# Attention with group norm: exponentials turned unnormalised, a sixth group turned by DMA, tile pairs parted into heads and tails

## What is computed

```python
y = group_norm(x, 4 groups) * gn_gamma + gn_beta
q, k, v = split(einsum('bchw,dc->bdhw', y, w_qkv) + b_qkv)
scores = einsum('bnc,bcm->bnm', q, k) * C ** (-0.5)
w = softmax(scores, axis=-1)
a = einsum('bnm,bmc->bnc', w, v)
return x + einsum('bchw,dc->bdhw', a, w_out) + b_out
```

## Time and profile before

| what | us |
|---|---|
| runs | 144.53, 144.81, 147.99 |
| median | 144.81 |
| span of the profiled execution | 143.7 |
| TensorE busy | 133.6 |
| VectorE busy | 103.9 |
| ScalarE busy | 67.7 |
| GpSimd busy | 57.1 |

### The profile page before, as it was taken

How to read it: one execution, slowest core, us unless ns; L and a number is a source line. 1 busy time by engine, 2 the same in 40 slices (tenths; PEclk the granted TensorE clock), 3 DMA queues, 4 the chain that set the end, 5 groups by cost and what they waited for, 6 DMA issues and landing times.

```text
span 143.7 us, 1862 instructions
## 1 busy us (share of the span) xinstructions
PE 133.6 (93%) x589; PEld 94.4 (66%) x589; DVE 103.9 (72%) x201; ACT 67.7 (47%) x122; POOL 57.1 (40%) x66
## 2 busy tenths in 40 slices
PE   7999999997499979997999999999999999999990
PEld 7978579873367635665655556766776666768770
DVE  0597587799978999899496987898763787463402
ACT  3164858763266526543361364455843666353000
POOL 6032347963334666633355556433543213330000
PEclk9999999999999999999999999999999999999998
DMA  4940000000045976983598539973996001000211
GB/s 159 310 188 0 0 5 0 0 2 0 0 101 117 206 165 141 206 200 109 109 203 197 152 66 206 206 182 81 212 203 168 0 0 73 0 0 0 80 70 73
DMA packets 6154, 15.07 MB, mean 105 GB/s; under 512 B 1664, under 2 KB 1664, under 8 KB 6144
## 3 DMA queue, kind: packets, MB, share of 16 engines
q1 hardware_dynamic: 5856, 14.69, 41.3%
q10 hardware_dynamic: 288, 0.27, 0.5%
HBM read 2.36 MB, written 2.10 MB: 31 GB/s over the span
## 4 chain that ended last, share of the span: by engine, by line
PE 66%; DVE 14%; SPq 7%; issue 5%; ACT 4%; DMA 2%; DVEq 0%
PE mixed L765 22%; SPq L235 7%; PE scores L715 5%; PE scores L714 5%; PE turned L731 5%; PE scores L717 5%; DVE scores L527 5%; PE scores L773 4%; DVE crossed L552 4%; ACT probs L366 3%; PE mixed L760 3%; PE mixed L762 3%; PE mixed L761 3%; PE turned L661 2%; PE mixed L661 2%
## 5 line engine op out<-in xcount | busy, mean ns | idle before, releaser
L295 POOL TENSOR_SCALAR probs<-probs,inv_sum 128x1024 f32<-128x1024 f32 x32 | 35.9, 1122 | 63.7 <-DVE inv_sum L532 63.7
L527 DVE TENSOR_SCALAR_CACHE_REDUCE scores<-scores,key_bias 128x1024 f32<-128x1024 f32 x31 | 40.0, 1289 | 13.9 <-PE scores L717 13.8
L366 ACT ACTIVATE probs<-scores,neg_max 128x1024 f32<-128x1024 f32 x32 | 35.7, 1115 | 18.7 <-DVE scores L527 17.7
L765 PE MATMUL mixed<-crossed,v 128*128 128x512 f32 x80 | 37.7, 593 | 1.0 <-DMA crossed<-crossed 1.0
L714 PE MATMUL scores<-y_hi,z_hi 128*128 128x512 f32 x62 | 34.6, 558 | 0.3 <-DVE z_lo L489 0.3
L552 DVE STREAM_TRANSPOSE crossed<-probs 128x1024 f32<-128x1024 f32 x20 | 24.8, 1241 | 0.0
L715 PE MATMUL scores<-y_lo,z_hi 128*128 128x512 f32 x62 | 24.4, 394 | 0.0
L765 PEld LDWEIGHTS mixed<-crossed,v 128*128 128x128 f32 x80 | 14.1, 190 | 11.6 <-issue 11.0
L717 PE MATMUL scores<-y_hi,z_lo 128*128 128x512 f32 x62 | 19.3, 392 | 0.0
L714 PEld LDWEIGHTS scores<-y_hi,z_hi 128*128 128x128 f32 x62 | 11.7, 189 | 8.8 <-issue 5.7
L715 PEld LDWEIGHTS scores<-y_lo,z_hi 128*128 128x128 f32 x62 | 11.7, 189 | 7.0 <-issue 5.5
(11 more groups left out here) (147 smaller groups left out, 168.9 us busy)
## 6 DMA issues: line engine op xcount, KB each, us to landing
crossed<-crossed SPq DMA_DIRECT2D x80, 128.0 KB, 2.3
out_dram<-result SPq DMA_DIRECT2D x8, 256.0 KB, 2.5
xs<-in_x_dram SPq DMA_DIRECT2D x2, 512.0 KB, 6.4
xs<-in_x_dram SPq DMA_DIRECT2D x3, 256.0 KB, 5.0
xs<-in_x_dram ACTq DMA_DIRECT2D x1, 256.0 KB, 3.5
ws<-in_weights_dram SPq DMA_DIRECT2D x1, 256.0 KB, 3.7
vecs<-in_vectors_dram ACTq DMA_DIRECT2D x1, 3.0 KB, 3.9
```

Source lines behind the costliest of these rows:

```text
L295: pool.tensor_scalar(probs[:, i % RING, :], probs[:, i % RING, :], inv_sum[:, i:i + 1], 1.0, ALU.mult, ALU.mult).then_inc(s_probs, 1)
L366: act.activation(probs[:, i % RING, :], scores[:, i % 2, :], ACT.Exp, bias=neg_max[:, i:i + 1], scale=-1.0, accum_out=row_sum[:, i:i + 1]) ...
L527: dve.tensor_scalar(scores[:, i % 2, :], scores[:, i % 2, :], key_bias[:, b % 2, i:i + 1], None, ALU.subtract, ALU.min, accum_out=neg_max[ ...
L765: mm = pe.matmul(bank, v[:, b % 2, k, :], at, start=first, stop=final)
```

## The change

The flips and the turning of group 0 wait for the exponentials alone. Groups 0 to 6 stay unnormalised until after the mix: one reciprocal for each group (`inverse_sums`), its 512 values are kept in DRAM (`keep_rows`) and read back on all partitions (`spread_rows`), `scale` multiplies the mixed tile by them, and GpSimd adds `x` with the output bias (`residual`, `add_residual`). Group 7 is normalised as before. Group 6 is swapped by DMA instead of turned by TensorE. In groups 1 to 6 the first pair of tiles is mixed in float32; each of the other three is parted: ScalarE makes the head (`pair_head`), GpSimd the tail in place (`pair_tail`), TensorE does three fp32r matmuls for a tile. All values get head and tail (`value_copy`, now two activations, and `value_tail`). The statistics of batches 2 and 3 are made together in blocks 0 to 3, their group means at block 6. y, z, and the big buffers become tensors of their own. The core of the diff:

```diff
-SWAPPED = range(1, 6)
-SPLIT_GROUPS = (6, 7)
-HOME = (0, 1, 0, 1, 0, 1)
+SWAPPED = range(1, 7)
+LAST = GROUPS_OF_FOUR - 1
+WHOLE_PAIR = 0
+PAIRS = KT // 2
+PARTED = PAIRS - 1
 SWAP = 16 * SQ * SQ
-MIX = {4: [(0, 1)], 5: [(0, 1)], 6: [(0, 1)], 7: [(0, 1)], 8: [(0, 1)], 9: [(0, 1)], 10: [(0, 2)],
-       27: [(5, 2)], 28: [(5, 3)], 29: [(5, 2)], 30: [(5, 1), (6, 3)], 31: [(6, 5)]}
-for group in range(1, 5):
-    for k, tiles in enumerate((3, 2, 1, 2) if group % 2 else (1, 2, 3, 2)):
-        MIX.setdefault(4 * group + 7 + k, []).append((group, tiles))
+MIX = {4: [(0, 1)], 5: [(0, 1)], 6: [(0, 1)], 7: [(0, 1)], 8: [(0, 1)], 9: [(0, 1)], 10: [(0, 2)]}
+for group in SWAPPED:
+    for k in range(PAIRS):
+        MIX.setdefault(4 * group + 7 + k, []).append((group, 2))
+
+inverse_rows = nc.dram_tensor("inverse_rows", (GROUPS_OF_FOUR - 1, HALF), fp32)
...
+def keep_rows(group):
+    sp.wait_ge(s_inv, group + 1)
+    sp.dma_start(inverse_rows[group].rearrange("(p u) -> p u", u=QB),
+                 inv_sum[:, group, :]).then_inc(s_rows[group % 2], 16)
+
+def spread_rows(group):
+    sp.wait_ge(s_rows[group % 2], 16 * (group // 2 + 1))
+    if group > 1:
+        sp.wait_ge(s_scaled, group - 1)
+    sp.dma_start(inv_wide[:, group % 2, :],
+                 inverse_rows[group].partition_broadcast(128)).then_inc(s_wide[group % 2], 16)
...
 sp.wait_ge(s_flipped, QB * group)
-if group > 1:
+if group > 2:
     sp.wait_ge(s_mixed, KT * (group - 1))
 for k in range(SQ):
     for g in (0, 2, 1, 3):
         t = g ^ k
-        sp.dma_start(crossed[32 * t:32 * t + 32, group % 2, g * N:(g + 1) * N],
-                     crossed[32 * g:32 * g + 32, 2 + group % 2, t * N:(t + 1) * N]
+        sp.dma_start(home[group % 2][32 * t:32 * t + 32, g * N:(g + 1) * N].bitcast(fp32),
+                     flipped[group % 2][32 * g:32 * g + 32, t * N:(t + 1) * N]
                      ).then_inc(s_swapped[group % 2], 16)
...
-swap(1)
-for group in range(2, 6):
+keep_rows(0)
+spread_rows(0)
+for group in SWAPPED:
+    keep_rows(group)
     swap(group)
-    store(group - 2)
-for group in range(4, GROUPS_OF_FOUR):
+    spread_rows(group)
+    if group >= 2:
+        store(group - 2)
+for group in range(5, GROUPS_OF_FOUR):
...
+def value_tail(b):
+    pool.wait_ge(s_v, 3 * (b + 1))
+    if b >= 2:
+        pool.wait_ge(s_mixed, KT * HALVES * (b - 1))
+    pool.tensor_tensor(v_lo[:, b % 2, :, :], v[:, b % 2, :, :], v_hi[:, b % 2, :, :].bitcast(fp32),
+                       ALU.subtract).then_inc(s_v_lo, 1)
+
+def pair_tail(group, pair):
+    pool.wait_ge(s_head, pair_number(group, pair))
+    there = pair_at_home(group, pair)
+    pool.tensor_tensor(there, there.bitcast(fp32), pair_of_heads(pair).bitcast(fp32),
+                       ALU.subtract).then_inc(s_parted, 1)
...
+def residual(b):
...
+pool.tensor_scalar(xs[:, b, :], xs[:, b, :], out_bias[:, :], 1.0,
+                   ALU.add, ALU.mult).then_inc(s_residual, 1)
...
+def add_residual(group):
+    b, g = group // HALVES, group % HALVES
+    pool.wait_ge(s_scaled, group + 1)
+    pool.wait_ge(s_residual, b + 1)
+    pool.tensor_tensor(result[:, g, :], result[:, g, :], xs[:, b, g * HALF:(g + 1) * HALF],
+                       ALU.add).then_inc(s_result, 1)
...
-normalise(0, 0)
 rstd_of(1, 2, 2)
-normalise(0, 1)
 for b in range(BATCHES):
     for i in range(BLOCKS):
-        behind = 0 < b < BATCHES - 1 and i == 3
-        if behind:
-            y_tail(b + 1, 0)
+        n = BLOCKS * b + i
+        group, pair = (n - 6) // QB, (n - 6) % QB
+        if group in SWAPPED and pair != WHOLE_PAIR:
+            pair_tail(group, pair)
+        if b == 0 and i == 0:
+            normalised_input(1)
         if b == 0 and i in (2, 3):
             y_tail(1, i - 2)
-        if after(b, i, 2)[0] < BATCHES:
-            normalise(*after(b, i, 2))
-        if behind:
+        if i == 2:
+            value_tail(b)
+        if i == 5:
+            residual(b)
+        if b == 1 and i == 0:
+            rstd_of(2, 4, 3)
+        if 0 < b < BATCHES - 1 and i == 1:
+            normalised_input(b + 1)
+        if 0 < b < BATCHES - 1 and i == 3:
+            y_tail(b + 1, 0)
+        if 0 < b < BATCHES - 1 and i == 4:
             y_tail(b + 1, 1)
-        if 0 < b < BATCHES - 1 and i == 0:
-            rstd_of(b + 1, b + 2, b + 2)
-        if i == (0 if b == 0 else 1) and b + 1 < BATCHES:
-            normalised_input(b + 1)
         if i == 7 and b + 1 < BATCHES:
             z_tail(b + 1)
+        if n >= 12 and n % QB == 0:
+            add_residual((n - 12) // QB)
+        if n + 2 >= QB * LAST and n + 2 < BATCHES * BLOCKS:
+            normalise(n + 2)
+for pair in range(2, PAIRS):
+    pair_tail(LAST - 1, pair)
+add_residual(LAST - 2)
+add_residual(LAST - 1)
...
+act.activation(v[:, b % 2, lo:hi, :], tiles, ACT.Copy)
+act.activation(v_hi[:, b % 2, lo:hi, :], tiles, ACT.Copy).then_inc(s_v, 1)
...
+def pair_head(group, pair):
+    act.wait_ge(s_swapped[group % 2], swaps(group))
+    act.wait_ge(s_mixed, KT * (group - 1) + 2 * (pair + 1) if group > 1 else KT)
+    act.activation(pair_of_heads(pair), pair_at_home(group, pair).bitcast(fp32), ACT.Copy).then_inc(s_head, 1)
...
+        group, pair = (BLOCKS * b + i - 6) // QB, (BLOCKS * b + i - 6) % QB
+        if group in SWAPPED and pair != WHOLE_PAIR:
+            pair_head(group, pair)
         if after(b, i, 2)[0] < BATCHES:
             exponentials(*after(b, i, 2))
         if i == (1 if b == 0 else 2) and not last:
             y_head(b + 1)
+for pair in range(2, PAIRS):
+    pair_head(LAST - 1, pair)
...
-def inverse_sum(b, i):
-    dve.wait_ge(s_exp, BLOCKS * b + i + 1)
-    dve.reciprocal(inv_sum[:, i:i + 1], row_sum[:, i:i + 1]).then_inc(s_inv, 1)
+def inverse_sums(group):
+    first = group % HALVES * QB
+    dve.wait_ge(s_exp, QB * (group + 1))
+    dve.reciprocal(inv_sum[:, group, :], row_sum[:, first:first + QB]).then_inc(s_inv, 1)
+
+def last_inverse_sum(n):
+    dve.wait_ge(s_exp, n + 1)
+    dve.reciprocal(inv_sum[:, LAST, n % QB:n % QB + 1],
+                   row_sum[:, n % BLOCKS:n % BLOCKS + 1]).then_inc(s_inv_last, 1)
...
-dve.wait_ge(s_probs, n + 1)
+dve.wait_ge(s_exp, n + 1)
...
-def results(group):
+def scale(group):
     b, g = group // HALVES, group % HALVES
     dve.wait_ge(s_mixed, KT * (group + 1))
     if b >= 1:
         dve.wait_ge(s_stored[g], 16 * b)
-    dve.scalar_tensor_tensor(out=result[:, g, :], in0=mixed[:, g, :], scalar=out_bias[:, :],
-                             in1=xs[:, b, g * HALF:(g + 1) * HALF], op0=ALU.add,
-                             op1=ALU.add).then_inc(s_result, 1)
+    dve.wait_ge(s_wide[g], 16 * (b + 1))
+    dve.tensor_tensor(result[:, g, :].rearrange("p (u q) -> p u q", u=QB),
+                      mixed[:, g, :].rearrange("p (u q) -> p u q", u=QB),
+                      inv_wide[:, g, :].rearrange("p (q u) -> p u q", u=QB), ALU.mult).then_inc(s_scaled, 1)
...
+if (BLOCKS * b + i) % QB == 2 and (BLOCKS * b + i) // QB < LAST:
+    inverse_sums((BLOCKS * b + i) // QB)
...
-            results((BLOCKS * b + i - 11) // QB)
-        if ahead[0] < BATCHES:
-            inverse_sum(*ahead)
-        if b + 2 < BATCHES and i in (4, 5):
-            half_stats(b + 2, i - 4)
-            if i == 5:
-                channel_stats(b + 2, b + 3)
-        if 0 < b < BATCHES - 1 and i == 1:
-            dve.wait_ge(s_negated, b)
-            coefficients(b + 1, b + 2, b + 2, negated_mean[:, b + 1:b + 2])
-results(GROUPS_OF_FOUR - 2)
-results(GROUPS_OF_FOUR - 1)
+            scale((BLOCKS * b + i - 11) // QB)
+        if ahead[0] < BATCHES and BLOCKS * b + i + 2 >= QB * LAST:
+            last_inverse_sum(BLOCKS * b + i + 2)
+        if b == 0 and i < 4:
+            half_stats(2 + i // 2, i % 2)
+            if i == 3:
+                channel_stats(2, 4)
+        if b == 1 and i == 1:
+            dve.wait_ge(s_negated, 1)
+            coefficients(2, 4, 3, negated_mean[:, 2:4])
+scale(LAST - 1)
+last_result()
...
-pe.wait_ge(s_probs, n + 1)
+if n < QB:
+    pe.wait_ge(s_exp, n + 1)
+else:
+    pe.wait_ge(s_probs, n - QB * LAST + 1)
...
+pair = k // 2
+if group in SWAPPED and pair != WHOLE_PAIR and k % 2 == 0:
+    pe.wait_ge(s_parted, pair_number(group, pair))
 first, final = k == 0, k == KT - 1
-if group in SPLIT_GROUPS:
-    head, tail = PT_HI[group][:, k, :], PT_LO[group][:, k, :]
-    pe.matmul(bank, v_hi[:, k, :], head, start=first, stop=False)
-    pe.matmul(bank, v_hi[:, k, :], tail, start=False, stop=False)
-    mm = pe.matmul(bank, v_lo[:, k, :], head, start=False, stop=final)
-elif group in SWAPPED:
-    at = crossed[:, HOME[group], :].rearrange("p (g v u c) -> p v u g c", g=SQ, v=KT, u=QB)[:, k, :, :, :]
-    mm = pe.matmul(bank, v[:, b % 2, k, :], at, start=first, stop=final)
+if group == 0:
+    mm = pe.matmul(bank, v[:, 0, k, :], first_turned[:, k, :], start=first, stop=final)
+elif group == LAST:
+    pe.matmul(bank, v_hi[:, b % 2, k, :], last_head[:, k, :], start=first, stop=False)
```

(34 more changed lines are left out.)

209 lines of the change are left out of this document (115 added, 94 removed).

## The result

| kernel | median us (runs) | ratio to before, 95% interval | span of the profile |
|---|---|---|---|
| before | 144.94 (144.53 to 147.99) | | 143.7 |
| changed | 155.71 (155.18 to 156.36) | 1.074 [1.068, 1.080] | 154.0 |

The change makes the kernel 7.4% slower. The forecast was 154.3 us with 146.5 to 160: right in sign, 1.4 us low.

What follows compares the result with a forecast made beforehand. It took TensorE to bound the kernel before and late GpSimd tails to delay it after. First mix at 52.65, plus 76.2 of TensorE work and 21.05 of waits, gives 149.9; with 3.3 and 1.1, 154.3 us, range 146.5 to 160.

Steps and rivals of the forecast that it cites:

- What bounds, and the change of the bound: TensorE bounds before, 85.24 busy of 86.65 us; after, it waits for GpSimd's pair tails and at Z0, about 20 us.
- The tail: GpSimd's pair tail, two inputs and 1024 columns: 2.33 us each, within bounds of 1.12 and 2.56.
- The walk through the queues: Block by block from 11 through ScalarE, GpSimd and TensorE queues: waits of 21.05 us; blocks 15 to 23 take 32.55.
- First mix to last matmul: TensorE from first transfer-fed mix at 52.65 to last matmul at 149.9: 76.2 us of work plus 21.05 of waits.
- The start: Stretch up to the first transfer-fed mix: flip(7) ends about 39.0 instead of 40.2, so that mix starts at 52.65.
- eight reciprocals leave: VectorE in blocks 4 and 5: eight reciprocals, and statistics of 0.68 us each, are no longer there.
- the first transfer-fed mix at 52 to 54: Sign of the forecast on TensorE: the first mix fed by transfers starts at 52 to 54 us.
- A: Rival: tails ready before their block, TensorE stays the bound; 135 to 138 us, needs tails well under 1.6; chance 0.09.
- B: Rival: half of the coupling, heads or tails shorter, tails 1.75 to 2.0 us; time 142 to 147.5; chance 0.12.
- C: Rival: GpSimd's tails collide with VectorE's two-input work on GpSimd's port; at 2.56 a tail, 159 us; chance 0.07.
- D: Rival: gaps of 2.6 us lower TensorE's clock to 1.2 GHz, up to 7 us more before the end; 161; chance 0.04.
- clock 1.00: Sign of the forecast: TensorE's granted clock stays at 1.00, that is 2.4 GHz.

Runs made afterwards that it cites:

- half tails: Changed kernel with each GpSimd pair tail cut from 1024 to 512 columns, order kept, output not the reference's; 139.45 us, ratio 0.962 to before.

## Why the prediction was right, point by point

- **What bounds, and the change of the bound**: right. TensorE's waits went to pair tails and to Z0, by name, and the last chain is GpSimd's (34%) as much as TensorE's (33%).
- **The tail, 2.33 us from two rows of the same operation**: measured 2.374 and 2.380. The bounds 1.12 and 2.56 were far apart, and the value taken was 2% off. The Trainium skill (GPSIMD Engine Reference, section 3.1) led to an estimate of 2.2; the row decides, and the rule is 7% low here.
- **The walk through the queues**: right in kind, and in size within 3%. Blocks 15 to 23: 32.55 predicted, 33.50 measured. Each of the places that it named is in the trace: Z0 behind the tail, pair 2 of an odd group behind Z0's copy, pair 1 of an even group behind two copies (1.14 idle at 74.03, 1.2 predicted), and three tails in a row before the last group with idle times of 2.48, 0.64 and 0.65 (2.55, 0.95 and 0.95 predicted from start to start).
- **First mix to last matmul**: 97.25 predicted, 99.94 measured (50.69 to 150.63). Of the 2.7, tails 0.045 longer along a path with some 20 of them are 0.9, an estimate; the lower clock about 131 is 0.7. In block 19 the tail of pair 1 of group 3 waited 0.67 for its head, which stood behind an exponential and y's head, and started 4.18 us behind the last mix of group 2 where the walk had 3.75: 0.4. The other 0.7 are left open.
- **The start**: mis-sized. The first transfer-fed mix was put at 52.65 and came at 50.69. Of the 2.0, the flip of block 7 ended 1.1 earlier than worked out, with the first transfer at 37.91 instead of 39.0; the chain of transfers took 12.8 in place of 13.6. Both vary from one execution to the next, the first transfer from 37.83 to 38.78 and the mix from 49.83 to 51.87 in the ten profiles with this start, but none reaches 52.65. Much of the first part is the reciprocals. The prediction counted eight instructions of 0.16, but in the kernel before each of them also holds up VectorE's queue until its exponential is through. Ahead of four of the first five VectorE sat idle for it, 1.44, 0.71, 0.60 and 0.73 us; ahead of the later ones it didn't. The longest:

```profile
18.07 0.16 DVE L532 RECIPROCAL inv_sum<-row_sum 128x1 f32<-128x1 f32 x1 [1.44 <-ACT probs L366]
18.15 0.73 DVE L509 SCALAR_TENSOR_TENSOR z_lo<-mixed,z_bias,z_hi 128x512 fp32r<-128x512 f32 x1
...
19.18 1.28 DVE L527 TENSOR_SCALAR_CACHE_REDUCE scores<-scores,key_bias 128x1024 f32<-128x1024 f32 x1
```

  and in the changed kernel:

```profile
16.89 0.75 DVE L599 SCALAR_TENSOR_TENSOR z_lo_even<-mixed,z_bias,z_hi_even 128x512 fp32r<-128x512 f32 x1 [0.73 <-ACT z_hi_even L507]
...
17.93 1.28 DVE L617 TENSOR_SCALAR_CACHE_REDUCE scores<-scores,key_bias 128x1024 f32<-128x1024 f32 x1
```

  The reciprocal is gone from there, z_lo starts 1.26 earlier, and the second maximum 1.25. The lead then changes with the statistics, which now lie in blocks 0 to 3: the first four flips start 1.5, 0.8, 1.5 and 2.3 us earlier than before. That the 1.25 are still part of the last is argued, not tested. The term that was mis-sized is "eight reciprocals leave": the rule that a wait delays all that is queued behind it was applied to ScalarE and GpSimd and forgotten on VectorE. With it one of the prediction's signs failed, the first transfer-fed mix at 52 to 54.
- **GpSimd's busy time**: near 90 predicted, 90.4. **The scale**: 0.7 predicted, 1.055 measured; hidden, as said.
- **The ends**: span 153.2 predicted, 154.0; the median of the runs lies 1.7 over the span (the profiled execution itself took 155.81), and 1.1 was taken from before, from a median and the span of one execution that needn't be the same; the runs of before beside the experiments lie 1.8 over their spans too (145.52 and 143.7). The errors cancelled in part: start −2.0, stage behind it +2.7, store +0.1, distance to the span +0.6, sum 1.4. That the middle is off by only 1.4 us is thus partly luck; that the kernel is slower, and by which waits, is not.
- **The rivals.** A and B didn't come about; half tails show that A's condition was put rightly. C wasn't active (no pair tail over 2.41). D was held to be unlikely because the clock had stayed at 1.00 across the gap of 2.6 in the earlier trace rows. That inference was wrong: the clock fell at about 131, after gaps of only 0.7 and 1.2 us in the stretch before, and then stayed at 1.00 across the 2.48 before group 6, where the rival had put it. It cost 0.7 us of the path, not 7, and the sign "clock 1.00" failed with it. The four executions don't show the cost: 155.61 at a clock of 1.000, 155.81 and 156.36 at 0.989, 155.18 at 0.974.
- **Left open**: whether the sixth group by transfer and the scaling would pay without the statistics moved. No run tried them apart.
